# Spread tiles of a factorisation-machine layer fetched by DMA from a DRAM scratch, four to a transfer, in place of selection matmuls on TensorE

## The reference

```
z = jnp.einsum('bhd,bkd,hks->bsd', x0, xk, W) + b[None, :, None]
z = jax.nn.relu(z)
```

## Time and profile before

| what | value |
|---|---|
| runs of the kernel | 2995.06, 2996.9, 2997.92 us, median 2996.9 |
| span of the profiled execution | 2989.2 us, first to last instruction |
| what lies around the span | 5.9 to 8.7 us, 7.7 at the median (the page gives no time of its own for the profiled execution) |
| PE busy | 2879.6 us, 96% |
| DVE busy | 2752.8 us, 92% |
| ACT busy | 1724.0 us, 58% |
| POOL busy | 1628.9 us, 54% |
| DMA | 16.17 MB in all, 5 GB/s over the span |

### The profile page before, as it was taken

The page is one execution under the profiler, slowest core; times in us unless marked ns, Lnnn a source line. Parts: engine busy times, 40 slices in busy tenths (PEclk is TensorE's granted clock), DMA queues, the critical chain, the costliest instruction groups (busy, mean ns, idle before and its releaser), DMA issues.

```text
span 2989.2 us, 32998 instructions
## 1 busy us (share of the span) xinstructions
PE 2879.6 (96%) x9666; PEld 1773.7 (59%) x9666; DVE 2752.8 (92%) x2461; ACT 1724.0 (58%) x1733; POOL 1628.9 (54%) x644
## 2 busy tenths in 40 slices
PE   1999999999999999999999999999999999999988
PEld 0566665666666666666566666666666666666646
DVE  3599999999999999999999999999999999999983
ACT  0466655566655556665556666555666555566634
POOL 7448194783819566381965639396572948700000
PEclk9899999999999999999999999999999999999999
DMA  2000000000000000000000000000000000000000
GB/s 63 4 3 3 3 3 5 2 5 2 2 3 2 5 3 4 1 3 3 2 5 3 4 1 2 4 2 5 3 4 1 2 5 2 5 0 0 2 19 29
DMA packets 35184, 16.17 MB, mean 5 GB/s; under 512 B 17023, under 2 KB 33520, under 8 KB 35008
## 3 DMA queue, kind: packets, MB, share of 16 engines
q0 software_dynamic: 19968, 5.15, 2.0%
q1 hardware_dynamic: 11752, 7.61, 1.0%
q10 hardware_dynamic: 3367, 2.48, 0.3%
HBM read 13.09 MB, written 2.11 MB: 5 GB/s over the span
## 4 chain that ended last, share of the span: by engine, by line
PE 82%; ACT 6%; issue 5%; DVE 4%; ACTq 0%; POOL 0%; DMA 0%; SPq 0%; DVEq 0%
PE zacc_a L781 31%; PE zacc_b L781 26%; PE side_a L827 6%; PE side_b L827 6%; PE zacc_a L814 6%; PE zacc_b L814 5%; DVE prod L681 3%; ACT spread L508 2%; ACT high L527 1%; ACT direct L491 1%; ACT maps L490 1%; ACT maps L489 1%; DVE low L654 1%; DVE sums L690 1%; PE side_a L836 0%
## 5 line engine op out<-in xcount | busy, mean ns | idle before, releaser
L429 POOL DMA_INDIRECT landed<-in_tbl,rows_id x624 | 1527.4, 2448 | 203.8 <-issue 199.7
L681 DVE TENSOR_TENSOR prod<-spread,maps 128x1024 f32<-128x1024 f32 (+1 forms) x1280 | 1506.2, 1212 | 29.1 <-PE zacc_b L814 16.3
L527 ACT ACTIVATE high<-prod 128x1024 fp32r<-128x1024 f32 (+2 forms) x736 | 776.7, 1055 | 752.1 <-DVE prod L681 504.9
L654 DVE TENSOR_TENSOR low<-prod,high 128x1024 fp32r<-128x1024 f32 (+1 forms) x672 | 814.6, 1212 | 22.8 <-ACT high L527 22.7
L781 PE MATMUL zacc_a<-prod,w_plain 128*128 128x512 f32 (+2 forms) x1536 | 720.6, 594 | 0.0
L781 PE MATMUL zacc_b<-prod,w_plain 128*128 128x512 f32 (+2 forms) x1536 | 718.2, 593 | 0.0
L450 POOL TENSOR_TENSOR mark<-mark 128x1 f32<-128x1 f32 x15 | 101.1, 6743 | 770.7 <-DVE rows_split L608 697.0
L781 PEld LDWEIGHTS zacc_a<-prod,w_plain 128*128 128x128 f32 (+2 forms) x1536 | 289.7, 189 | 231.1 <-issue 201.2
L781 PEld LDWEIGHTS zacc_b<-prod,w_plain 128*128 128x128 f32 (+2 forms) x1536 | 289.1, 189 | 230.5 <-issue 197.0
L508 ACT ACTIVATE spread<-side_a 128x1024 f32<-128x1024 f32 x320 | 326.8, 1021 | 101.2 <-PE side_a L827 100.4
L508 ACT ACTIVATE spread<-side_b 128x1024 f32<-128x1024 f32 x320 | 327.0, 1022 | 89.3 <-PE side_b L827 78.1
(11 more groups left out here) (110 smaller groups left out, 1811.8 us busy)
## 6 DMA issues: line engine op xcount, KB each, us to landing
landed<-in_tbl,rows_id POOLq DMA_INDIRECT x624
features<-feat ACTq DMA_DIRECT2D x16, 128.0 KB, 1.7
spread<-features SPq DMA_DIRECT2D x4, 512.0 KB, 5.3
spread<-in_pick SPq DMA_DIRECT2D x1, 856.8 KB
spread<-in_W_top SPq DMA_DIRECT2D x1, 512.0 KB, 4.1
rows_id<-in_ids SPq DMA_DIRECT2D x16, 19.5 KB, 1.7
spread<-in_W_top SPq DMA_DIRECT2D x2, 128.0 KB, 2.8
spread<-in_W_top SPq DMA_DIRECT2D x1, 256.0 KB, 2.9
```

The lines of the kernel that those rows point to most:

```text
L429: nc.gpsimd.indirect_dma_start(out=landed[:, f, :], out_offset=None, in_=tables[f], in_offset=bass.IndirectOffsetOnAxis(ap=rows_id[:, f:f ...
L527: nc.scalar.activation(high[0:rows, h, :], prod[0:rows, p, :], ACT.Copy).then_inc(s_round, 1)
L654: nc.vector.tensor_tensor(to, whole, top, ALU.subtract).then_inc(s_lowv, 1)
L681: nc.vector.tensor_tensor(to, spread[0:rows, t, :], maps[0:rows, :], ALU.mult).then_inc(s_prod, 1)
```

## The change

- The gathered rows of a group are transposed on PE in plain fp32 for both its chunks at once (`turn_x`, at tile 13 of every even turn), and ACT copies them to `x` (39 partitions x 1024 columns for each chunk, at tile 15).
- At tile 16 of every even turn, two turns ahead, SP writes them to DRAM, for each of the two chunks: `x_copies`, 8 copies of every field in the order of the spread tiles (two transfers with 160 rows of 4 KB), and `x_periods`, 4 copies of the 39 fields in a row (156 rows of 4 KB).
- SP loads back, per chunk: `x_thrice` (3 transfers of 39 rows) and `shifted` (7 of 117 or 78 rows, in a ring of 4 slots), which take the place of PSUM in SQUARED; and `spread` in five transfers of 128 x 16 KB (2 MiB, four tiles), each issued when DVE has made the LAST product with the fourth of its tiles.
- `side_work` is gone from PE with all its selection matmuls, and so are ACT's 20 spread copies and the splitting of gathered rows.
- `PLAN` has 30 F tiles and 17 V tiles.
- POOL gathers a group in one run from tile 16 of an even turn, and SP's id load stands behind the writes.

```diff
...
-SPLIT = 2 * FIELDS
...
-PERIODIC = N1 * MAPS
-BACK = PERIODIC + TRIPLE + PER0 * (N0 - 1)
-PICK_W = BACK + TRIPLE
+EVEN = 2 * N1
+COPIES = 8
+PERIODS = 4
+PIECE = 4
+PIECES = N1 // PIECE
+RING0 = 4
...
-PLAN = "FVFVFVFFVFVFFVFVFVFVFVFFFVFVFVFVFVVFVFVVFVFVFVV"
+PLAN = "FVFFVFFVFFVFFVFFFVFV" "FVFVFVF" "FVFFVFFVFFVFFVFFFVFV"
...
-LAG = 2
...
-AHEAD = 4
-LOW_ROWS_AT, COPY_ROWS_AT = 42, 40
...
-TURN_AT, THRICE_AT = 3, 9
+TURN_AT, COPY_AT, WRITE_AT, GATHER_AT = 13, 15, 16, 16
...
-            with sp.Fori(1, GROUPS) as g:
-                sp.wait_ge(s_gather, g * (16 * FIELDS))
-                sp.dma_start(rows_id[:, :], ids[bass.ds(g * ROWS, ROWS), :]).then_inc(s_ids, 16)
+            def group_of(n):
+                return n.group(1, 0)
+            def write_x(n):
+                odd = n.odd
+                sp.wait_ge(s_x, n.count(1, 1))
+                for h in range(2):
+                    to = x_copies[bass.ds(group_of(n), 1), odd, h, :, :, :].rearrange("g i t c -> (g t) i c")
+                    sp.dma_start(to, x[h:EVEN:2, odd:odd + 1, :].to_broadcast([N1, COPIES, COLS])
+                                 ).then_inc(s_written[odd], 16)
+                to = x_periods[bass.ds(group_of(n), 1), odd, :, :, :].rearrange("g k f c -> (g f) k c")
+                sp.dma_start(to, x[0:FIELDS, odd:odd + 1, :].to_broadcast([FIELDS, PERIODS, COLS])
+                             ).then_inc(s_written[odd], 16)
+            def period(n, first, rows):
+                flat = x_periods[bass.ds(group_of(n), 1), n.odd, :, :, :].rearrange("g k f c -> (g k f) c")
+                return flat[first:first + rows, :]
+            def load_shifted(n, u):
+                rows = rows_of(N1 + u)
+                sp.dma_start(shifted[0:rows, u % RING0, :], period(n, PER0 * u, rows)).then_inc(s_shifted[u], 16)
+            def load_first(n):
+                sp.wait_ge(s_written[n.odd], n.group(48, 48))
+                for s in range(PER0):
+                    sp.dma_start(x_thrice[s * FIELDS:(s + 1) * FIELDS, :], period(n, FIELDS - s, FIELDS)
+                                 ).then_inc(s_thrice, 16)
+                for u in range(RING0):
+                    load_shifted(n, u)
+            def load_spread(n, q):
+                src = x_copies[bass.ds(group_of(n), 1), n.odd, :, :, PIECE * q:PIECE * (q + 1), :]
+                src = src.rearrange("g h i t c -> (g h i) (t c)")
+                to = spread[:, PIECE * q:PIECE * (q + 1), :].rearrange("p t c -> p (t c)")
+                sp.dma_start(to, src.unsqueeze(1).to_broadcast([2 * COPIES, COPIES, PIECE * COLS])
+                             ).then_inc(s_spread[q], 16)
+            def emit(turn, j):
+                nxt, after = turn.shift(1), turn.shift(2)
+                if turn.fixed and turn.number() == -1 and j == 0:
+                    write_x(nxt)
+                    write_x(after)
+                    sp.wait_ge(s_gather, 16 * FIELDS)
+                    sp.dma_start(rows_id[:, :], ids[ROWS:2 * ROWS, :]).then_inc(s_ids, 16)
+                    load_first(nxt)
+                if j == WRITE_AT and not turn.odd and after.real():
+                    write_x(after)
+                    write_x(turn.shift(3))
+                    if turn.shift(4).real():
+                        sp.wait_ge(s_gather, after.group(16 * FIELDS, 16 * FIELDS))
+                        sp.dma_start(rows_id[:, :], ids[bass.ds(after.group(ROWS, ROWS), ROWS), :]).then_inc(s_ids, 16)
+                u = j - N1 - 1 + RING0
+                if RING0 <= u < N0 and nxt.real():
+                    sp.wait_ge(s_square, nxt.count(N0, u - RING0 + 1))
+                    load_shifted(nxt, u)
+                if j == SQUARED[-1] and after.real():
+                    sp.wait_ge(s_square, nxt.count(N0, N0))
+                    load_first(after)
+                q = (j - LAST[0]) // PIECE
+                if j in LAST and (j - LAST[0]) % PIECE == PIECE - 1 and nxt.real():
+                    if turn.real():
+                        sp.wait_ge(s_prod, n_prod(turn, j) + 1)
+                    elif q == 0:
+                        sp.wait_ge(s_prep, 1)
+                    load_spread(nxt, q)
+            turns(sp, emit, GROUPS - 2)
...
+            def gather():
+                for f in range(FIELDS):
+                    nc.gpsimd.indirect_dma_start(
+                        out=landed[:, f, :], out_offset=None, in_=tables[f],
+                        in_offset=bass.IndirectOffsetOnAxis(ap=rows_id[:, f:f + 1], axis=0),
+                    ).then_inc(s_gather, 16)
...
+                    gather()
+                    pool.wait_ge(s_ids, 32)
+                    pool.wait_ge(s_turned, 2)
+                    gather()
+                fetched = turn.shift(4)
+                if j == GATHER_AT and not turn.odd and fetched.real():
+                    pool.wait_ge(s_ids, fetched.group(16, 16))
+                    pool.wait_ge(s_turned, fetched.count(1, 0))
+                    pool.wait_ge(s_mark, fetched.group(1, -1))
+                    nc.gpsimd.tensor_tensor(mark[:, 0:1], mark[:, 0:1], mark[:, 1:2], ALU.add).then_inc(s_mark, 1)
+                    gather()
...
+            def copy_x(n):
+                act.wait_ge(s_turned, n.count(1, 1))
+                if not n.fixed or n.number() > 1:
+                    act.wait_ge(s_written[n.odd], n.group(48, 0))
+                nc.scalar.activation(x[0:FIELDS, n.odd, :], sides[n.odd][0:FIELDS, :], ACT.Copy).then_inc(s_x, 1)
...
-                    if j == TURN_AT + LAG:
...
-                    if j == THRICE_AT + LAG:
...
-                        take(turn, 0)
-                    t = j - N1 - N0 - LAG
-                    if 0 <= t:
-                        spread_tile(turn, t)
...
-                    spread_tile(last, N1 - LAG + j)
+                if j == COPY_AT and not turn.odd and turn.shift(2).real():
+                    copy_x(turn.shift(2))
+                    copy_x(turn.shift(3))
+                if nxt.real() and j == N1 + N0 - 1 + LZ:
+                    take(turn, 0)
...
                     take(turn, 1)
...
                 if j in SQUARED:
                     u, nxt = j - N1, turn.shift(1)
                     if u == 0:
-                        dve.wait_ge(s_thrice, nxt.count(1, 1))
-                    dve.wait_ge(s_side, n_side(nxt, SQUARE_X + u) + 1)
-                    nc.vector.tensor_tensor(to, side(nxt, SQUARE_X + u)[0:rows, :], x_thrice[0:rows, :],
+                        dve.wait_ge(s_thrice, nxt.count(16 * PER0, 16 * PER0))
+                    dve.wait_ge(s_shifted[u], nxt.count(16, 16))
+                    nc.vector.tensor_tensor(to, shifted[0:rows, u % RING0, :], x_thrice[0:rows, :],
                                             ALU.mult).then_inc(s_square, 1)
                     return
                 t = j if j in PAIRED else j - N1 - N0
                 if j in PAIRED:
                     if t == 0:
...
+            def turn_x(n):
+                if not n.odd:
+                    pe.wait_ge(s_gather, n.group(16 * FIELDS, 16 * FIELDS))
+                if not n.fixed or n.number() > 1:
+                    pe.wait_ge(s_x, n.count(1, -1))
+                nc.tensor.matmul(sides[n.odd][:, 0:2], ident[:, :], ident[:, 0:2], start=True, stop=True)
+                for d in range(CHAN):
+                    done = nc.tensor.transpose(sides[n.odd][0:FIELDS, d * ROWS:(d + 1) * ROWS],
+                                               landed[:, :, n.odd * CHAN + d], ident[:, :])
+                done.then_inc(s_turned, 1)
             def emit(turn, j):
                 if turn.fixed and turn.number() == -1 and j == 0:
-                    pe.wait_ge(s_pick, 1)
+                    pe.wait_ge(s_const, 16 * 4)
+                    turn_x(turn.shift(1))
+                    turn_x(turn.shift(2))
...
-                side_work(turn, j)
+                if j == TURN_AT and not turn.odd and turn.shift(2).real():
+                    turn_x(turn.shift(2))
+                    turn_x(turn.shift(3))```

PE in LAST and the tiles after it, before the change. `side_a` and `side_b` are the PSUM tiles of the selection matmuls; a row is one kind of matmul for both halves of the columns.

```order
99 L827 MATMUL side_a<-x_split,pick 128x512 x2
100 L781 MATMUL zacc_a<-prod,w_plain 128x512 x2
101 L827 MATMUL side_b<-x_split,pick 128x512 x2
102 L781 MATMUL zacc_a<-high,w_low 128x512 x2
103 L781 MATMUL zacc_a<-high,w_high 128x512 x2
104 L814 MATMUL zacc_a<-low,w_high 128x512 x2
105 L827 MATMUL side_a<-x_split,pick 128x512 x2
```

165 lines of the change are left out of this document (29 added, 136 removed).

## The result

| | before | after |
|---|---|---|
| median of the runs | 2997.4 us | 3203.2 us |
| all runs | 2995.1 to 3015.5 | 3189.6 to 3220.6 |
| span of the profiled run | 2989.2 | 3204.3 |

The ratio is 1.066 (95% interval 1.061 to 1.072): the change makes the kernel slower by 6.6%. The forecast of 2903 us was wrong: the time lies far above its range of 2800 to 2966. What it called "the other side" happened, and went further than its 3020.

What follows compares the result with a forecast made beforehand. PE bounded the kernel before, DVE close behind; DVE would bound it after. Span 2989.2 - 338 saved + 222 write stalls + 22 start = 2895, 2903 us with the time around it; own range 2800 to 2966, 8-in-10 range 2740 to 3020.

Steps and rivals of the forecast that it cites:

- the other side: Rival: writes at the pace of few partitions, stall over 19 us in even turns, up to 3020 us; chance 0.19.
- The price of DVE: DVE's work after the change: 76.8 us a turn, 154.6 for two turns with small waits, making it the bound.
- PE's price list: PE's start-to-start times: F tile 1.72 us, pair 0.46 to 0.47, eight transposes 0.55; 75.8 us a turn after.
- The idle PE: PE would run at a lower clock for some us behind each stall; priced at nothing, DVE being the bound.
- The writes: Even-turn writes ahead of shift 4: 4.38 MB at 190 GB/s, 23.1 us; DVE stalls 14.8 us, 222 in all.
- the sum: Forecast's addition: 2989.2 - 338 saved + 222 of stalls + 22 at the start = 2895 us as a span.
- the rule of the ports: Trainium skill: DMA bandwidth follows SBUF ports reached; estimated 29 us for the writes and a stall of about 22.
- The start of the writes: From the end of DVE's product 13 until SP may write in an even turn: 5.9 us.
- The gathers: POOL's gathers, 95 us a group from tile 16, end some 45 us before they are due; priced at nothing.
- The spread fetch: Loading the spread pieces each turn is hidden from 235 GB/s up; priced at nothing; chance of being late 0.07.
- The start: Before the loop settles, first writes, loads and the second group's gathers cost 22 us more (5 to 54).
- The case past 19 us of stall: Rival of writes at few partitions' pace; even turns eat all the gain at 21 us, 149 GB/s; chance 0.19.

Runs made afterwards that it cites:

- w_narrow: Changed kernel, its loop writes taken from a constant tile with the same bytes and partitions, all loads reading the first group's data; 3183.6 us, for comparison only.
- w_strided: As w_narrow, but the write sources are every sixth and every third partition of 0 to 117, same bytes; 3028.1 us.
- w_wide: As w_narrow, but each write takes all 128 partitions, 5 KB of each, 3.9 MB in all; 2856.4 us.
- e1: Changed kernel with SP loading the next group's ids ahead of the six writes instead of behind them; 3157.5 us, ratio 1.049 to the kernel before.

## Why the prediction was wrong

**The price of DVE: right.** Two turns without a new wait are 154.6 us, as forecast. DVE's busy time was to be 2460 us and is 2510; the 2460 are 32 turns alone, and before the change too 32 turns (2694) lie 59 us under the page's 2752.8. PE's price list can't be read as cleanly, since PE ran at two clocks.

**The idle PE, priced at nothing: right.** In the stall the clock is 0.50, the 1.2 GHz level, and 0.70 in the window right behind, while DVE, the bound, is busy 10.00 of that window's 10.00 us.

**The writes: the step that failed.** The prediction said: "I take 190 GB/s, midway between the last two, since the writes start from 39 partitions". The 4.38 MB took from 1504.23 + 1.7 to 1540.92, 35.0 us, which is 125 GB/s, under the lowest row that bounded it (157). The term in its place is 35.0 and not 23.1: 11.9 us of stall more. Two things are in it. The windows above show 5.1 MB moved in that time, since shifts 5 and 6 move at the same time, where the sum let them follow; and even with them the burst runs at 140 GB/s. w_narrow against w_strided shows that the narrow sources make about half of the stall, and w_wide that most of the rest lies in the form of the writes. The 157 came from 78 partitions, so it was no lower end for 39; only the rule of the ports gave a lower one, and it had been kept out of the sum and the range.

**The start of the writes: "5.9" was 10.2.** From the end of product 13 (1494.07) to the first write (1504.23) it took 4.3 us more, and PE's wait for the gathers is 4.12. The two misses make 16.2 us, of which 11.8 show in the stall (26.6 for 14.8), as DVE comes to the fifth SQUARED product some 4.3 later too, mostly through its wait of 3.37 on `spread` in between.

**The gathers, "priced at nothing": wrong.** They were to end 45 us ahead of need, but start 36 us behind the first write (1504.23 to 1540.39): 15 us go into issuing the six writes, 20 into the landing of the ids. And a group takes 117 us of POOL, not 95 (3002 ns each, 2448 in the earlier trace rows; why is not shown). They then hold the transposes up, which closes a second ring in the changed kernel. e1 opened it and gained 1.8%: behind it the first ring, of the burst and the shifts, is nearly as long.

**The spread fetch: nearly hidden.** 212 GB/s is under the 235 that hiding needs; the waits beyond the start are 103.3 - 37.9 = 65 us.

**The start: 22 was 44** (181.19 less 136.8), by the same two rates.

**The sum again.** To 2895 come 177 us of stalls (436.3 less 37 at the start is 399, for 222), 65 of spread waits, 22 at the start and 23 of DVE waiting for ACT: 3182 of 3204.3. The other 22 were not put down to anything, nor is all of the 23 new: before, DVE waits 22.7 for ACT too, 15.8 of it at the start.

**The chances.** The case past 19 us of stall held 0.19. Its breakeven, 149 GB/s, stood below the slowest row, and this was read as evidence against it. But that row was a transfer from twice as many partitions, so it spoke for the case as much as against it.

## What to carry to other kernels

A DMA's rate is no property of the chip to be taken from another row. Here it went by where the SBUF side lies (few neighbouring partitions were slow) and by how many outer rows the access pattern has; price a new transfer from a row with the same shape, and if there is none let the range reach well below the slowest. Before one row is copied in DRAM for a broadcast, try the broadcast as the outermost dimension of a DMA: here that took away most of a burst. A burst also delays what stands behind it in its queue and what only shares the engines, so follow small loads such as the ids through the ring that they feed.
